# Perceiver block with a routed expert layer: six of eight inner slices of each looped expert's output as split products, and its copy out of PSUM moved to ScalarE

## The chip, the cores and the metric

The kernel runs on one core of a Trainium2 chip. The metric is the device time of one execution in microseconds (us); smaller is better. Of several runs the median counts.

## What is computed

The reference is one block of a perceiver on x of 8 x 64 x 512 with a context of 8 x 512 x 512, all in f32: a cross attention with its own output projection, a causal self attention (16 heads of 32) with a convolution over its output, and an expert layer. The expert layer is the part that matters here:

```
logits = x @ gate_w.T ; probs = softmax(logits) ; top2_p, top2_i = top_k(probs, 2)
w = top2_p / max(sum(top2_p), 1e-10)
hh = gelu(einsum('nd,edf->nef', x, w1) + b1)        # E = 14 experts, F = 1024
all_out = einsum('nef,efd->ned', hh, w2) + b2       # D = 512
moe = w[:, 0:1] * out0 + w[:, 1:2] * out1           # of the two chosen experts
x = x + clip(layernorm(x) + moe, -100, 100)
```

There are 512 tokens, so 1024 pairs of token and expert.

## The kernel before

Tokens are sorted by expert through a table in DRAM, `rows_dram`, in blocks of 128 rows. Each expert has at least one block; here there are 14 blocks, numbered b = 0 to 13, worked in pairs, u = b % 2 naming the buffer. For a block, TensorE turns the gathered rows (`turn_x`, L1901, with the transposes of L1522), multiplies them by w1 (`hidden`, L1906), turns the result so that the inner dimension of 1024 lies on partitions (`turn_hidden`, L1928, matmuls of L1933), and multiplies by w2 (`output`, L1936). The inner dimension comes in FT = 8 slices of 128.

An f32 product can be made in two ways. Unsplit it is one f32 matmul, which the profile counts as two instructions. Split it is three matmuls of the rounded type fp32r: high x high, high x low and low x high, where the high part is a copy of the tile to fp32r (ScalarE) and the low part the tile minus its high part (VectorE). The hidden products (L1920 to L1922) are all split. For outputs, blocks 0, 1 and the last are unsplit (L1943, L2002), and the others, 2 to 12, go through `split_output` (L1949): slices G to 7 unsplit (L1953) and slices 0 to G-1 split (L1958 to L1960), with G = 4. All of it adds up in one PSUM bank, YP.

The steady state is a loop over pairs on each engine. Within one iteration, for block b of the pair, the order is written out by hand:

- TensorE (L1984): turn_x(b), output(b-2), turn_hidden(b-1), hidden(b).
- ScalarE (L772): split_hi (L644, four high parts of w1 of block b, L648), high_w2 (L741, two high parts of w2 of block b-1, L746; it waits until that w2 has landed), store_y (L752: waits for y_taken, issues the store of block b-2 at L755), gelu (L726: eight activations of block b-1, L732, then the high part of its split slices, L739).
- VectorE (L1461): take_xT (L1334, L1336: high and low part of the turned x), split_lo (L1314, four low parts of w1, L1319), take_y (L1435: waits for y_psum and for y_free, then copies YP to ysb, L1438), low_w2 (L1422, two low parts, L1427), low_h (L1430, waits for the high part of h, L1432), take_h (L1402, two copies of the hidden result out of PSUM, L1407; waits for the end of hidden(b)).
- SyncE (L449) issues the loads: x rows of block b (L453) after turn_x(b-2), w2 of block b-2 (L446) when output(b-4) has ended, w1 of block b (L459) when hidden(b-2) has ended. A load of w1 or w2 is 2 MB.
- GpSimd issues the load of b1 (L881).

The semaphores that matter: y_psum counts ended outputs, y_taken the copies out of YP, y_free the stores of ysb that have landed, w2_high and w2_low the parts of w2, h_high and h_low those of h, hi_ready and lo_ready those of w1. TensorE waits in split_output for both w2_low of the block and for h_low behind the unsplit slices.

After the loop come output(12), with turn_hidden(13) placed inside it, the output of block 13 in two halves, and the gathers of all rows (L889) by GpSimd, which wait for the stores of the blocks. Block 13 is added from SBUF by a matmul with a matrix `last_w` that is made by VectorE during output(12).

Buffers are cut out of larger ones: w2_hi lies in wqkv_lo and c_hi, h_hi in A2r, last_w in wqkv, att and attT are tiles of their own from the cross attention.

Of the kernel before, what the change touches and what calls it, by code (L numbers as in the profile page):

```python
# [14 lines left out]
F32 = mybir.dt.float32  # L15
# [4 lines left out]
ALU = mybir.AluOpType  # L20
ACT = mybir.ActivationFunctionType
AX = mybir.AxisListType

P = 128
B, S = 8, 64
D = 512
Q = 512
KT = D // P
N = B * S
NT = N // P  # L30
# [3 lines left out]
FT = F // P  # L34
# [14 lines left out]
def perceiver_kernel(nc, t, out):  # L49

    ctx = ExitStack()
    with ctx:
        def sb(name, shape, dt=F32):
            return ctx.enter_context(nc.sbuf_tensor(name, shape, dt))

        def overlaid(name, rounded_name, shape):

            with nc.sbuf_tensor(name, shape, F32) as plain:
                pass
            return plain, sb(rounded_name, shape, F32R)  # L60

        def sem(name):
            return ctx.enter_context(nc.semaphore(name))
# [36 lines left out]
        w2, w2_lo = overlaid("w2", "w2_lo", [P, 2, FT * D])  # L100
# [11 lines left out]
        c_raw, c_hi = overlaid("c_raw", "c_hi", [P, KT, N])  # L112
# [10 lines left out]
        wqkv_flat = wqkv[:, :, :].rearrange("p k n -> p (k n)")  # L123
        wqkv_lo_flat = wqkv_lo[:, :, :].rearrange("p k n -> p (k n)")
        got = wqkv_flat[:, 0:2 * NT * D].rearrange("p (t c d) -> p t c d", t=NT, c=2)

        last_w = wqkv_flat[:, 4096:4608].rearrange("p (t s) -> p t s", t=NT)
        last_wT = wqkv_flat[:, 5120:5632].rearrange("p (t n) -> p t n", t=NT)
        A2, A2r = overlaid("A2", "A2r", [P, 3 * KT * N + KT * B * (S + 2)])
        zero_rows = A2[:, 7680:8192]  # L130
        cwT = A2[:, 0:2048].rearrange("p (k n) -> p k n", k=KT)
# [25 lines left out]
        hpre = A2[:, 2048:3072]  # L157
        hT = A2[:, 3072:5120].rearrange("p (u f n) -> p u f n", u=2, f=FT)
        ysb = A2[:, 5120:6144].rearrange("p (u d) -> p u d", u=2)
        att = sb("att", [P, Q])  # L160

        attT = sb("attT", [P, KT, P]); c2q = sb("c2q", [P, D])
        slot_row_i = c2q[:, 0:P].bitcast(I32); last_w2 = c2q[:, P:2 * P]
        over_e, over_r = (c2q[:, at:at + E * MORE] for at in (2 * P, 2 * P + P // 2))
        over_e_i, over_r_i = over_e.bitcast(I32), over_r.bitcast(I32)
# [21 lines left out]
        slot_c = sb("slot_c", [P, 2, E]); key = sb("key", [P, E, MORE]); base_slot = sb("base_slot", [P, 1])  # L187
        slot_k = sb("slot_k", [P, 2, NT]); slot_i = sb("slot_i", [P, 2, NT], I32)
        rank = sb("rank", [P, 2]); rel = sb("rel", [P, 2, NT]); early = sb("early", [P, 2, NT]); wgot = sb("wgot", [P, 2, NT])
        G = FT // 2  # L190
        w2_hi = [wqkv_lo_flat[:, 0:G * D], c_hi[:, :, :].rearrange("p k n -> p (k n)")[:, 0:G * D]]
        h_hi = A2r[:, 1024:2048].rearrange("p (u f n) -> p u f n", u=2, f=G)
        h_lo = A2r[:, 3072:5120].rearrange("p (u f n) -> p u f n", u=2, f=FT)[:, :, 0:G, :]
        c_hi_flat = c_hi[:, :, :].rearrange("p k n -> p (k n)")
        c_raw_flat = c_raw[:, :, :].rearrange("p k n -> p (k n)")
# [27 lines left out]
        HP, HT, XT, YP = (pb[0:2], pb[2:4]), pb[4:6], pb[6], pb[7]  # L223
# [58 lines left out]
        hT_psum, gelu_done, y_psum = map(sem, ("hT_psum", "gelu_done", "y_psum"))  # L282

        y_taken = sem("y_taken")
        gelu_half, h_high, h_low = sem("gelu_half"), sem("h_high"), sem("h_low")
        w2_high, w2_low = sem("w2_high"), sem("w2_low")

        y_free = [sem(f"y_free{u}") for u in range(2)]
# [68 lines left out]
        def rows_of(eng, b):  # L357

            return eng.value_load(blk_i[0:1, 1, bass.ds(b, 1)], min_val=0, max_val=ROW_BLOCKS - 1)
# [116 lines left out]
        def _(act):  # L476
# [249 lines left out]
            def gelu(b, u, loaded, first=False):  # L726

                act.wait_ge(hT_psum, b + 1)
                for f in range(FT):
                    if f == 0:  # L730
                        act.wait_ge(b1_in[u], loaded)
                    ins = nc.scalar.activation(hT[:, u, f, :], HT[f // 4][:, tile(f % 4)], ACT.Gelu,  # L732
                                               bias=b1_sb[:, u, f:f + 1])
                    if f == G - 1 and not first:
                        ins.then_inc(gelu_half, 1)
                ins.then_inc(gelu_done, 1)
                if not first:
                    act.wait_ge(gelu_half, b + 1)
                    nc.scalar.activation(h_hi[:, u], hT[:, u, 0:G, :], ACT.Copy).then_inc(h_high, 1)  # L739

            def high_w2(b, u, loaded):  # L741

                act.wait_ge(w2_in[u], loaded)
                for i in range(2):
                    at = slice(i * G * D // 2, (i + 1) * G * D // 2)
                    nc.scalar.activation(w2_hi[u][:, at], w2[:, u, at], ACT.Copy).then_inc(w2_high, 1)  # L746

            def store_first(b, u):
                act.wait_ge(y_taken, b + 2)
                act.dma_start(rows_dram[b * P:(b + 1) * P, :], ysb[:, u, :]).then_inc(y_free[u], 16)  # L750

            def store_y(b, u):  # L752
                row = rows_of(act, b)
                act.wait_ge(y_taken, b + 2)
                act.dma_start(rows_dram.rearrange("(b p) d -> b p d", p=P)[bass.ds(row, 1)]  # L755
                              .rearrange("o p d -> p (o d)"), ysb[:, u, :]).then_inc(y_free[u], 16)
# [5 lines left out]
            act.wait_ge(scattered, 16 * 2 * NT)  # L762
            store_first(0, 0)
            gelu(1, 1, 16, True)
            for count, n in ((gelu_half, 2), (h_high, 2), (w2_high, 4)):
                act.sem_inc(count, n)
            split_hi(1, w1_in[1], 16, range(2, KT))
            store_first(1, 1)
# [3 lines left out]
            with act.Fori(2, pairs) as i:  # L772
                for u in range(2):
                    split_hi(u, w1_in[u], 16 * i, range(KT))
                    if u == 0:
                        high_w2(2 * i - 1, 1, 16 * i)
                    else:
                        high_w2(2 * i, 0, 16 * i + 16)
                    store_y(2 * i - 2 + u, u)
                    if u == 0:  # L780
                        gelu(2 * i - 1, 1, 16 * i)
                    else:
                        gelu(2 * i, 0, 16 * i + 16)
# [115 lines left out]
        def _(dve):  # L899
# [521 lines left out]

            def low_w2(b, u):  # L1422

                for i in range(2):
                    dve.wait_ge(w2_high, 2 * b + i + 1)
                    at = slice(i * G * D // 2, (i + 1) * G * D // 2)
                    nc.vector.tensor_tensor(w2_lo[:, u, at], w2[:, u, at], w2_hi[u][:, at].bitcast(F32), ALU.subtract) \  # L1427
                        .then_inc(w2_low, 1)

            def low_h(b, u):  # L1430
                dve.wait_ge(h_high, b + 1)
                nc.vector.tensor_tensor(h_lo[:, u], hT[:, u, 0:G, :], h_hi[:, u].bitcast(F32), ALU.subtract) \  # L1432
                    .then_inc(h_low, 1)

            def take_y(b, u, turn):  # L1435
                dve.wait_ge(y_psum, b + 3)
                dve.wait_ge(y_free[u], 16 * turn)
                nc.vector.tensor_copy(ysb[:, u, :], YP[:, :]).then_inc(y_taken, 1)  # L1438
# [13 lines left out]
            split_lo(3, 1, range(KT))  # L1452
            take_xT(3, 1)
            take_y(1, 1, 1)
            for count, n in ((h_low, 2), (w2_low, 4)):
                dve.sem_inc(count, n)
            low_w2(2, 0)
            low_h(2, 0)
# [2 lines left out]
            with dve.Fori(2, pairs) as i:  # L1461
                for u in range(2):
                    take_xT(2 * i + u, u)
                    split_lo(2 * i + u, u, range(KT))
                    take_y(2 * i + u - 2, u, i)
                    low_w2(2 * i + u - 1, 1 - u)
                    low_h(2 * i + u - 1, 1 - u)
                    take_h(2 * i + u, u)
# [8 lines left out]
            for n in range(NT):  # L1477
# [4 lines left out]
                ins = nc.vector.tensor_tensor(last_w[:, n, :], last_w[:, n, :], last_w2[:, :], ALU.add)  # L1482
# [33 lines left out]
        def _(pe):  # L1516
            mm = nc.tensor.matmul
# [430 lines left out]

            def split_output(onto, b, u, at, width, between=None):  # L1949
                for f in range(G, FT):  # L1950
                    if between and f == G + 2:
                        between()
                    mm(onto, hT[:, u, f, :], w2[:, u, f * D + at:f * D + at + width], start=(f == G), stop=False)  # L1953
                pe.wait_ge(w2_low, 2 * b + 2)
                pe.wait_ge(h_low, b + 1)
                for f in range(G):
                    cols = slice(f * D + at, f * D + at + width)
                    mm(onto, h_hi[:, u, f, :], w2_hi[u][:, cols], start=False, stop=False)  # L1958
                    mm(onto, h_hi[:, u, f, :], w2_lo[:, u, cols], start=False, stop=False)
                    ins = mm(onto, h_lo[:, u, f, :], w2_hi[u][:, cols], start=False, stop=(f == G - 1))  # L1960
                return ins

            pe.sem_inc(y_psum, 2)
# [7 lines left out]
            for n in range(NT):  # L1971
                ins = nc.tensor.transpose(XT[0:E, tile(n)], wsel[:, n, :], ident[:, :])
# [21 lines left out]
            for n in range(NT):  # L1994
                ins = nc.tensor.transpose(XT[:, tile(n)], last_w[:, n, :], ident[:, :])
# [3 lines left out]
            for c in range(2):  # L1999
                for f in range(FT):  # L2000
                    at = f * D + c * D // 2
                    ins = mm(HALF[c], hT[:, 1, f, :], w2[:, 1, at:at + D // 2], start=(f == 0), stop=(f == FT - 1))  # L2002
                ins.then_inc(half_psum, 1)

            for n in range(NT):
# [3 lines left out]
                for c in range(2):  # L2009
                    if n == 0:  # L2010
# [3 lines left out]
                    ins = mm(pb[n][:, half], last_wT[:, n, :], ysb[:, 1, half], start=False, stop=True,  # L2014
                             skip_group_check=True)
# [43 lines left out]
```

## Time and profile before

| | us |
|---|---|
| median of 3 runs | 454.69 |
| lowest and highest of them | 451.72, 455.02 |
| the profiled execution, own time | 455.08 |
| its span, first to last instruction | 453.5 |
| busy in the span: TensorE, VectorE, ScalarE, GpSimd | 416.2, 320.4, 195.2, 66.4 |
| mean granted TensorE clock | 0.98 |

Busy times overlap; weight loads (PEld) run beside the matmuls (PE). The times of matmuls are modelled at their ends, so their issue distance is read from the chain of waits, where each piece lasts until the next one begins, and not from the mean of one. The chain is followed back from the last instruction to whatever released it.

### The profile page before, as it was taken

To read this page: it belongs to the slowest core of one execution; us is meant where nothing else is said; L and a number is where in the kernel's file an instruction comes from. 1 tells how busy PE (TensorE), PEld (TensorE's weight loads), DVE (VectorE), ACT (ScalarE), POOL (GpSimd) and SP (SyncE) were. 2 spreads that over 40 slices of the span, in tenths; PEclk is the share of its full clock that TensorE was granted. 3 is DMA by queue.
4 is the path that set the end of the run, shared out by engine and by line. 5 is a ranking of instruction groups with operands and counts; after the bars stand their busy time and mean duration, and the time that the engine had idled before them with its cause. 6 is when DMAs were issued, how large, how long until landed. Compare 5 with 4: busy or idle time off the path is not lost.

```text
span 453.5 us, 8173 instructions
## 1 busy us (share of the span) xinstructions
PE 416.2 (92%) x3051; PEld 311.3 (69%) x3060; DVE 320.4 (71%) x605; ACT 195.2 (43%) x347; POOL 66.4 (15%) x80
## 2 busy tenths in 40 slices
PE   1999999999999899997868999999999999999980
PEld 1666466689897798974547856777777777777740
DVE  5759787684189835428866986887888877778537
ACT  4236134123257143135226151957666667674200
POOL 2210000002216300211112500000000000000074
PEclk9999999999999899999889999999999999999996
DMA  7998798999902800047051559999999999994243
GB/s 257 401 375 330 243 417 332 408 408 407 399 17 49 300 4 3 1 159 309 1 185 73 204 176 397 343 353 353 354 356 367 390 365 354 359 339 152 96 142 136
DMA packets 50814, 116.95 MB, mean 258 GB/s; under 512 B 3266, under 2 KB 3282, under 8 KB 50784
## 3 DMA queue, kind: packets, MB, share of 16 engines
q1 hardware_dynamic: 38176, 92.28, 55.5%
q10 hardware_dynamic: 10592, 19.41, 11.2%
q0 software_dynamic: 2016, 4.84, 3.3%
q8 instruction: 21, 0.34, 0.3%
q14 instruction: 9, 0.07, 0.0%
HBM read 93.98 MB, written 21.50 MB: 255 GB/s over the span
## 4 chain that ended last, share of the span: by engine, by line
PE 80%; DVE 10%; issue 3%; POOL 2%; DMA 2%; ACT 2%; DVEq 0%; ACTq 0%; POOLq 0%
PE banks L1953 8%; PE banks L1920 5%; PE banks L1922 5%; PE banks L1921 5%; PE banks L1554 4%; PE banks L1556 3%; PE banks L1555 3%; PE banks L1541 3%; PE banks L1593 3%; PE banks L1522 3%; PE banks L1692 3%; PE banks L1770 3%; PE banks L1693 3%; PE banks L1694 3%; PE banks L1933 2%
## 5 line engine op out<-in xcount | busy, mean ns | idle before, releaser
L1319 DVE TENSOR_TENSOR w_lo<-w,w_hi 128x1024 fp32r<-128x1024 f32 x48 | 55.5, 1217 | 0.0
L648 ACT ACTIVATE w_hi<-w 128x1024 fp32r<-128x1024 f32 x48 | 47.4, 1096 | 2.3 <-DMA w<-in_w 2.3
L732 ACT ACTIVATE A<-banks,b_sb 128x128 f32<-128x128 f32 x112 | 30.4, 383 | 37.1 <-DVE A L1438 21.6
L1920 PE MATMUL banks<-w_hi,cT_r 128*128 128x512 f32 x100 | 40.1, 401 | 0.6 <-DVE cT_r L1336 0.6
L1953 PE MATMUL banks<-w,A 128*128 128x512 f32 x88 | 39.7, 592 | 0.0
L1922 PE MATMUL banks<-w_hi,cT_r 128*128 128x512 f32 x100 | 39.0, 390 | 0.0
L1921 PE MATMUL banks<-w_lo,cT_r 128*128 128x512 f32 x100 | 39.0, 390 | 0.0
L1407 DVE COPY A<-banks 128x512 f32<-128x512 f32 x28 | 18.0, 685 | 16.6 <-PE banks L1922 16.6
L1694 PE MATMUL banks<-A2r,w_lo 128*128 128x256 f32 x96 | 28.0, 292 | 0.0
L833 POOL TENSOR_TENSOR A<-A,hrec 128x1024 f32<-128x1024 f32 x8 | 17.0, 2128 | 70.1 <-DVE hrec L1159 70.1
L881 POOL DMA_DIRECT2D b_sb<-in_b1T x12 | 6.5, 542 | 140.8 <-ACT A L732 133.9
L1953 PEld LDWEIGHTS banks<-w,A 128*128 128x128 f32 x88 | 15.9, 190 | 15.4 <-issue 15.3
L1554 PE MATMUL banks<-w_lo,A2r 128*128 128x512 f32 x52 | 22.5, 433 | 2.1 <-DVE A2r L1017 2.1
L746 ACT ACTIVATE wqkv_lo<-w 128x1024 fp32r<-128x1024 f32 x12 | 12.1, 1053 | 23.7 <-DMA w<-in_w 14.5
L1920 PEld LDWEIGHTS banks<-w_hi,cT_r 128*128 128x128 f32 x100 | 18.8, 188 | 4.3 <-DVE cT_r L1336 0.9
L1922 PEld LDWEIGHTS banks<-w_hi,cT_r 128*128 128x128 f32 x100 | 18.8, 188 | 4.0
L1556 PE MATMUL banks<-w_lo,A2r 128*128 128x512 f32 x52 | 21.3, 409 | 0.0
L1555 PE MATMUL banks<-w_lo,A2r 128*128 128x512 f32 x52 | 21.3, 409 | 0.0
L1921 PEld LDWEIGHTS banks<-w_lo,cT_r 128*128 128x128 f32 x100 | 18.8, 188 | 3.5
L1150 DVE TENSOR_REDUCE hmax<-banks 128x16 f32<-128x1024 f32 x8 | 9.8, 1223 | 14.8 <-PE banks L1722 14.8
L1668 PE MATMUL banks<-c_hi,w_lo 128*128 128x256 f32 x64 | 18.6, 291 | 0.5 <-DVE A2r L1057 0.5
L1694 PEld LDWEIGHTS banks<-A2r,w_lo 128*128 128x128 f32 x96 | 18.9, 197 | 0.0
(332 smaller groups left out, 1027.8 us busy)
## 6 DMA issues: line engine op xcount, KB each, us to landing
w<-in_w SPq DMA_DIRECT2D x24, 2048.0 KB, 9.6
rows_dram<-A ACTq DMA_DIRECT2D x1, 14592.0 KB, 45.8
A<-in_ctxT SPq DMA_DIRECT2D x8, 1024.0 KB, 10.4
A<-in_ctx SPq DMA_DIRECT2D x8, 1024.0 KB, 9.5
w<-in_w SPq DMA_DIRECT2D x5, 1024.0 KB, 6.1
rows_dram<-A ACTq DMA_DIRECT2D x13, 256.0 KB, 6.8
w<-in_wlT SPq DMA_DIRECT2D x3, 1024.0 KB, 14.7
wqkv<-in_wqkvT SPq DMA_DIRECT2D x1, 3072.0 KB, 16.1
```

Of the source, the lines that this page charges most:

```text
L648: nc.scalar.activation(w1_hi[:, u, k * F:(k + 1) * F], w1[:, u, k * F:(k + 1) * F], ACT.Copy).then_inc(hi_ready, 1)
L732: ins = nc.scalar.activation(hT[:, u, f, :], HT[f // 4][:, tile(f % 4)], ACT.Gelu, bias=b1_sb[:, u, f:f + 1])
L1319: nc.vector.tensor_tensor(w1_lo[:, u, part], w1[:, u, part], w1_hi[:, u, part].bitcast(F32), ALU.subtract).then_inc(lo_ready, 1)
L1554: mm(Z[n][:, :], high[:, k, :], wl_hi[:, at, :], start=(part == 0 and k == 0), stop=False)
L1555: mm(Z[n][:, :], high[:, k, :], wl_lo[:, at, :], start=False, stop=False)
L1556: ins = mm(Z[n][:, :], low[:, k, :], wl_hi[:, at, :], start=False, stop=(part == 2 and k == KT - 1))
L1668: mm(onto, w_hi, c_hi[:, k, tokens], start=(k == 0), stop=False)
L1694: ins = mm(onto, conv_lo[:, KT * tap + k, tile(f)], high, start=False, stop=(tap == CONV_ORDER[-1] and k == KT - 1))
L1920: mm(HP[u][c][:, :], xr[:, 0, u, k, :], high[:, at], start=(i == 0), stop=False)
L1921: mm(HP[u][c][:, :], xr[:, 0, u, k, :], low[:, at], start=False, stop=False)
L1922: ins = mm(HP[u][c][:, :], xr[:, 1, u, k, :], high[:, at], start=False, stop=(i == KT - 1))
L1953: mm(onto, hT[:, u, f, :], w2[:, u, f * D + at:f * D + at + width], start=(f == G), stop=False)
```

## The change

For blocks 2 to 12, slices 0 to 5 are split (G = 6) and slices 6 and 7 stay unsplit. The high and low parts of w2 become three copies and three subtractions of 128x1024 per block (CH = 3) in place of two; the high and low part of h go from 128x512 to 128x768. TensorE waits for w2_low ahead of every second split slice, and not once for all. In the loop, the copy of YP to ysb goes from VectorE (take_y, between split_lo and low_w2) to ScalarE, in store_y, between high_w2 and gelu. The copies of blocks 0, 1 and 12 stay on VectorE. In the last split output, turn_hidden stands between the two unsplit slices and the split ones. The parts find room in other buffers: w2_hi in three pieces per u, h_hi of u = 1 over att, last_w in c_raw.

```diff
@@ buffers @@
-        last_w = wqkv_flat[:, 4096:4608].rearrange("p (t s) -> p t s", t=NT)
-        last_wT = wqkv_flat[:, 5120:5632].rearrange("p (t n) -> p t n", t=NT)
+        c_flat = c_raw[:, :, :].rearrange("p k n -> p (k n)")
+        last_w = c_flat[:, 0:512].rearrange("p (t s) -> p t s", t=NT)
+        last_wT = c_flat[:, 1024:1536].rearrange("p (t n) -> p t n", t=NT)
...
-        att = sb("att", [P, Q])
-
-        attT = sb("attT", [P, KT, P]); c2q = sb("c2q", [P, D])
+        att_f, att_r = overlaid("att_f", "att_r", [P, 2 * Q])
+        att = att_f[:, 0:Q]
+        attT = att_f[:, Q:2 * Q].rearrange("p (k n) -> p k n", k=KT); c2q = sb("c2q", [P, D])
...
-        G = FT // 2
-        w2_hi = [wqkv_lo_flat[:, 0:G * D], c_hi[:, :, :].rearrange("p k n -> p (k n)")[:, 0:G * D]]
-        h_hi = A2r[:, 1024:2048].rearrange("p (u f n) -> p u f n", u=2, f=G)
+        G = 3 * FT // 4
+        CH = G // 2
+        c_hi_all = c_hi[:, :, :].rearrange("p k n -> p (k n)")
+        w2_hi = [[A2r[:, 6144:7168], A2r[:, 7168:8192], wqkv_lo_flat[:, 4096:5120]],
+                 [c_hi_all[:, 0:1024], c_hi_all[:, 1024:2048], wqkv_lo_flat[:, 5120:6144]]]
+        h_hi = [v[:, 0:G * P].rearrange("p (f n) -> p f n", f=G) for v in (A2r[:, 1024:2048], att_r[:, :])]
@@ ScalarE @@
-                    nc.scalar.activation(h_hi[:, u], hT[:, u, 0:G, :], ACT.Copy).then_inc(h_high, 1)
+                    nc.scalar.activation(h_hi[u], hT[:, u, 0:G, :], ACT.Copy).then_inc(h_high, 1)
...
-                for i in range(2):
-                    at = slice(i * G * D // 2, (i + 1) * G * D // 2)
-                    nc.scalar.activation(w2_hi[u][:, at], w2[:, u, at], ACT.Copy).then_inc(w2_high, 1)
+                for i in range(CH):
+                    at = slice(2 * i * D, 2 * (i + 1) * D)
+                    nc.scalar.activation(w2_hi[u][i], w2[:, u, at], ACT.Copy).then_inc(w2_high, 1)
...
-            def store_y(b, u):
+            def store_y(b, u, turn=None):
                 row = rows_of(act, b)
+                if turn is not None:
+                    act.wait_ge(y_psum, b + 3)
+                    act.wait_ge(y_free[u], 16 * turn)
+                    nc.scalar.activation(ysb[:, u, :], YP[:, :], ACT.Copy).then_inc(y_taken, 1)
                 act.wait_ge(y_taken, b + 2)
...
-                    store_y(2 * i - 2 + u, u)
+                    store_y(2 * i - 2 + u, u, i)
@@ VectorE @@
-                for i in range(2):
-                    dve.wait_ge(w2_high, 2 * b + i + 1)
-                    at = slice(i * G * D // 2, (i + 1) * G * D // 2)
-                    nc.vector.tensor_tensor(w2_lo[:, u, at], w2[:, u, at], w2_hi[u][:, at].bitcast(F32), ALU.subtract) \
+                for i in range(CH):
+                    dve.wait_ge(w2_high, CH * b + i + 1)
+                    at = slice(2 * i * D, 2 * (i + 1) * D)
+                    nc.vector.tensor_tensor(w2_lo[:, u, at], w2[:, u, at], w2_hi[u][i].bitcast(F32), ALU.subtract) \
                         .then_inc(w2_low, 1)
...
-                    take_y(2 * i + u - 2, u, i)
@@ TensorE @@
                 for f in range(G, FT):
-                    if between and f == G + 2:
-                        between()
                     mm(onto, hT[:, u, f, :], w2[:, u, f * D + at:f * D + at + width], start=(f == G), stop=False)
-                pe.wait_ge(w2_low, 2 * b + 2)
+                if between:
+                    between()
                 pe.wait_ge(h_low, b + 1)
                 for f in range(G):
+                    if f % 2 == 0:
+                        pe.wait_ge(w2_low, CH * b + f // 2 + 1)
```

The counts that are set ahead of the loop (`sem_inc` of w2_high and w2_low) go from 4 to 2 * CH, and the three split matmuls read the pieces of w2_hi.

## Rows read from the trace of the kernel before

**Rows 1.** Busy time by stretch: the expert loop, then single blocks of it
```profile
core 0: us, PE busy (x) PEld busy (x) DVE busy (x) ACT busy (x) POOL busy (x), PEclk, DMA share, GB/s
288.50:425.50 137.00, 137.00 (x592) 99.74 (x591) 112.92 (x140) 86.49 (x158) 4.96 (x10) 1.00 0.91 333
314.46:327.44 12.98, 12.98 (x58) 9.50 (x57) 10.68 (x12) 8.48 (x17) 0.54 (x1) 1.00 1.01 362
353.40:366.38 12.98, 12.98 (x58) 9.50 (x57) 10.68 (x12) 8.49 (x17) 0.54 (x1) 1.00 0.94 356
```

**Rows 2.** The chain of waits through one block: start us, us, what
```profile
321.10 0.87 PE banks L1933 x8
...
327.44 0.44 PE banks L1522 x4
327.87 3.44 PE banks L1953 x8
331.31 0.23 PE banks L1958
...
331.77 0.24 PE banks L1960
...
334.08 0.87 PE banks L1933 x8
...
340.42 0.11 PE banks L1522
```

**Rows 3.** Costliest groups, all stretches: busy us, mean ns of one | idle before
```profile
L1953 PE MATMUL banks<-w,A 128*128 128x512 f32 x88 | 39.7, 592 | 0.0
L746 ACT ACTIVATE wqkv_lo<-w 128x1024 fp32r<-128x1024 f32 x12 | 12.1, 1053 | 23.7 <-DMA w<-in_w 14.5 <-DVE A L1438 9.1
L739 ACT ACTIVATE A2r<-A 128x512 fp32r<-128x512 f32 x11 | 7.5, 681 | 0.0
L487 ACT ACTIVATE cT<-banks 128x512 f32<-128x512 f32 x8 | 4.7, 594 | 26.7 <-PE banks L1522 26.7
L1427 DVE TENSOR_TENSOR w_lo<-w,wqkv_lo 128x1024 fp32r<-128x1024 f32 x10 | 11.8, 1216 | 0.0
```

**Rows 4.** ScalarE and VectorE in order of time, one block of the loop
```profile
332.09 2.01 ACT L746 ACTIVATE wqkv_lo<-w 128x1024 fp32r<-128x1024 f32 x2 [2.76 <-DMA w<-in_w]
335.83 2.17 ACT L732 ACTIVATE A<-banks,b_sb 128x128 f32<-128x128 f32 x8 [1.73 <-DVE A L1438]
337.84 0.68 ACT L739 ACTIVATE A2r<-A 128x512 fp32r<-128x512 f32 x1
334.54 0.69 DVE L1438 COPY A<-banks 128x512 f32<-128x512 f32 x1
335.14 2.35 DVE L1427 TENSOR_TENSOR w_lo<-w,wqkv_lo 128x1024 fp32r<-128x1024 f32 x2
338.56 0.69 DVE L1432 TENSOR_TENSOR A2r<-A,A2r 128x512 fp32r<-128x512 f32 x1 [1.06 <-ACT A2r L739]
340.45 0.69 DVE L1407 COPY A<-banks 128x512 f32<-128x512 f32 x1 [1.21 <-PE banks L1922]
```

**Rows 5.** Stretches of 0.65 us around the hole; landing of L446's loads
```profile
347.56:348.21 0.65, 0.65 (x6) 0.59 (x5) 0.65 (x3) 0.00 (x0) 0.00 (x0) 1.00 1.01 416
...
349.51:350.16 0.65, 0.65 (x5) 0.53 (x4) 0.65 (x1) 0.65 (x4) 0.00 (x0) 1.00 0.76 129
...
DMA to landing us min/median/max: 9.4/10.2/10.7
```

**Rows 6.** In order of time: entry of the loop, and its end
```profile
283.38 2.01 ACT L746 ACTIVATE wqkv_lo<-w 128x1024 fp32r<-128x1024 f32 x2 [9.14 <-DVE A L1438]
285.29 2.15 ACT L732 ACTIVATE A<-banks,b_sb 128x128 f32<-128x128 f32 x8
...
288.97 3.44 PE banks L1953 x8
...
425.51 0.69 DVE L1438 COPY A<-banks 128x512 f32<-128x512 f32 x1 [0.57 <-PE banks L1960]
```

More of the change, by code:

```diff
@@ L764, in _ @@
             gelu(1, 1, 16, True)
-            for count, n in ((gelu_half, 2), (h_high, 2), (w2_high, 4)):
+            for count, n in ((gelu_half, 2), (h_high, 2), (w2_high, 2 * CH)):
                 act.sem_inc(count, n)
@@ L1431, in low_h @@
                 dve.wait_ge(h_high, b + 1)
-                nc.vector.tensor_tensor(h_lo[:, u], hT[:, u, 0:G, :], h_hi[:, u].bitcast(F32), ALU.subtract) \
+                nc.vector.tensor_tensor(h_lo[:, u], hT[:, u, 0:G, :], h_hi[u].bitcast(F32), ALU.subtract) \
                     .then_inc(h_low, 1)
@@ L1454, in _ @@
             take_y(1, 1, 1)
-            for count, n in ((h_low, 2), (w2_low, 4)):
+            for count, n in ((h_low, 2), (w2_low, 2 * CH)):
                 dve.sem_inc(count, n)
@@ L1950, in split_output @@
                 for f in range(G, FT):
-                    if between and f == G + 2:
-                        between()
                     mm(onto, hT[:, u, f, :], w2[:, u, f * D + at:f * D + at + width], start=(f == G), stop=False)
-                pe.wait_ge(w2_low, 2 * b + 2)
+                if between:
+                    between()
                 pe.wait_ge(h_low, b + 1)
                 for f in range(G):
+                    if f % 2 == 0:
+                        pe.wait_ge(w2_low, CH * b + f // 2 + 1)
                     cols = slice(f * D + at, f * D + at + width)
-                    mm(onto, h_hi[:, u, f, :], w2_hi[u][:, cols], start=False, stop=False)
-                    mm(onto, h_hi[:, u, f, :], w2_lo[:, u, cols], start=False, stop=False)
-                    ins = mm(onto, h_lo[:, u, f, :], w2_hi[u][:, cols], start=False, stop=(f == G - 1))
+                    own = slice(f % 2 * D + at, f % 2 * D + at + width)
+                    mm(onto, h_hi[u][:, f, :], w2_hi[u][f // 2][:, own], start=False, stop=False)
+                    mm(onto, h_hi[u][:, f, :], w2_lo[:, u, cols], start=False, stop=False)
+                    ins = mm(onto, h_lo[:, u, f, :], w2_hi[u][f // 2][:, own], start=False, stop=(f == G - 1))
                 return ins
```

## The prediction

> **What bounds the kernel now.** Read the stretches first. In the expert loop, about 288.5 to 425.5 us, TensorE is busy for all 137.00 us at granted clock 1.00, and one block takes 12.98 us of which TensorE fills 12.98, VectorE 10.68 and ScalarE 8.48 [rows 1]. So one matmul less is time less, as long as nobody else becomes late. The DMA engines show shares of 0.94 and 1.01 in two such blocks, at 356 and 362 GB/s [rows 1], which is the second suspect. Then read the chain of waits: inside a block it never leaves TensorE. It runs through the turn of x (0.44), the unsplit slices of the output (3.44), twelve split products (331.31 to 334.08), the turn of the hidden tile (0.87) and the hidden products (334.95, which is 334.08 + 0.87, to 340.42) [rows 2]. Last come the groups, for the price of each copy [rows 3], and the order of one block on ScalarE and VectorE, for the room beside TensorE [rows 4].
>
> **The change part by part.** *TensorE.* An unsplit slice is one f32 matmul that the profile counts as two instructions: 88 for 11 blocks of 4 slices [rows 3], so the split path runs 11 times (blocks 2 to 12). Four such slices take 3.44, one 0.86 [rows 2]. Twelve split products take 334.08 - 331.31 = 2.77, one 0.231, the three of a slice 0.693 [rows 2]. Two slices of a block go over from 0.86 to 0.693: -0.334 per block, and 11 x 0.334 = 3.67 us. Bounds: if each product ran at the pace of the hidden products (5.47 us for 24, 0.228 [rows 2]), eighteen would take 4.10 in place of 4.16 and the gain would be 0.39 a block, 4.3 in all; if the six new products of a block took the 0.24 of the slowest one in the chain [rows 2], they would cost 1.44 against 1.72, 0.28 a block, 3.1 in all. I take 3.67, since the new products are the same line, shapes and buffers' kind as the twelve. The waits on w2_low, now three instead of one, cost nothing by the hidden products, which wait for lo_ready ahead of every six and still keep 0.228. The turn of the hidden tile in the last split output stays behind two unsplit slices (f = 6, 7 in place of 4, 5), as before.
>
> *ScalarE* gets per block a third copy of w2 (two take 2.01, one 1.05, so 0.96 more [rows 3, 4]), the copy out of PSUM and a longer high copy of h. A 128x512 copy out of PSUM takes 0.594 on ScalarE [rows 3] against 0.69 on VectorE [rows 4]. The high copy of h goes from 128x512 (0.681) to 128x768; between 0.681 and the 1.053 of 128x1024 I take 0.87 [rows 3]. Sum 8.48 + 0.96 + 0.60 + 0.19 = 10.23 of the new 12.65. *VectorE* loses the copy (0.69), gets a third subtraction (2.35 for two, 1.22 for one alone, so 1.13 more) and a low part of h of 128x768 (0.69 now, 1.22 for 1024 elements, 0.96 taken) [rows 3, 4]: 10.68 - 0.69 + 1.13 + 0.27 = 11.39 of 12.65. Both fit, with 2.4 and 1.25 us to spare; the order must fit too.
>
> *The added wait.* ScalarE now waits for y_psum ahead of gelu, but it waited already there for VectorE's copy through y_taken: L732's idle time ends with L1438 (1.73 us) [rows 4]. Behind it are queued the store, gelu, the high part of h and the next split of w1; VectorE waits for the high part of h, TensorE for both. The loop puts high_w2 ahead of the copy, and high_w2 waits for a transfer. That is where the move can cost. Take the block of [rows 4], with its output ending at 334.08 before, and at 333.75 counted from the previous block's output end (321.10) and the new period. w2 lands at 332.09; three copies end at 335.06; the PSUM copy ends at 335.66 (before: 335.23); gelu began 0.60 behind that copy's end, so 336.26, and takes 2.17 to 338.43; the high part begins 0.16 before that and ends 339.14; VectorE's low part begins 0.04 after that and ends at 340.14. The hidden products end at 333.75 + 6.34 = 340.09, and take_h, 0.03 behind them before, is then 0.05 behind. So VectorE's two idle gaps of 1.06 and 1.21 us shrink, the second to nothing, and TensorE needs the low part only after 340.09 + 0.44 + 1.72 = 342.25. That leaves 2.1 us. Before it was over 5, since four unsplit slices stood ahead. A take_h that is later by some tenths costs nothing: its reader comes a whole output later, and the first low part of w1 is made near 343.8, where the hidden products that read it begin at 347.3.
>
> *Queues.* SP's waits are unchanged, the SP loads are issued by TensorE's progress and so 0.33 closer together; the y store leaves ScalarE's queue some 0.8 us later against the output's end, and its buffer is needed two blocks on. *DMA.* A block moves 362 GB/s x 12.98 us = 4.70 MB. Ahead of the hole that each block has, the rate stands at 416 GB/s; then four pieces of 0.65 us are lower, down to 129, when w1 has nearly landed and the next w2 has only been issued [rows 5]. At 400 GB/s the 4.70 MB need 11.75 us, so 12.65 fits, and the hole gets shorter. From issue to landing w2 takes 9.4 to 10.7 us [rows 5].
>
> *Entry.* The first split block has less room. The copies of w2 begin at 283.38 and the chain of ScalarE follows them with no gap [rows 6]: gelu 0.96 later, ends 288.4, the high part 289.1, VectorE's low part 290.1. TensorE starts output 2 at 288.97 and wants the low part at 290.69. It holds by 0.6 us; if not, the loss is once, under 1 us. *End.* The store of block 12 and the gathers hang on the end of output 12 (y copy at 425.51, released by L1960 [rows 6]), so what the loop gains arrives at the end. Moving last_w to another buffer and the overlays of att cost no instruction.
>
> **Sum.** The profiled run took 455.08 (span 453.5 plus 1.58 around it) and stands 0.39 above the median of 454.69. 455.08 - 3.67 = 451.41; on the median's footing 451.0.
>
> **The rivals.** *DMA rate holds the period.* The shares near 1.00 [rows 1] say that the engines are never without a packet; if bytes and not requests set the pace, the period stays 12.98, TensorE gets waits of 0.33 a block at the split of w2 or w1, and the time stays at 454.7. Against it stands the hole in the rate and the 416 beside it [rows 5]. The Trainium skill (DMA: Bandwidth & Descriptors, Where 436 GB/s comes from) is this rival's best advocate: it says that between HBM and SBUF the HBM side binds at about 358 GB/s per core, below the fabric's 435. By that price a block could not go under 13.1 us and nothing would be gained; this trace disagrees wherever it shows 416.
>
> *Late gelu: slower.* Ring through ScalarE: output ends, w2 is issued and lands 10.99 later, copies 2.97, PSUM copy 0.60, gap 0.60, gelu 2.01 to the high part, 0.87, low part 1.0, then eighteen products 4.16: 23.2 us for two periods of 12.65 = 25.3. It binds when w2 lands 2.1 us later than now, and makes the kernel slower than before from 2.8 us later (26.0 for two of 12.98). Landings 3.7 later, near 13.9 from issue, give (23.2 + 3.7) / 2 = 13.45 a block and 454.7 + 10 x 0.47 = 459.4. For it: the loads come closer together on engines at share 1.00, and the copy out of PSUM, gelu and h all stand behind that landing now. Against: in ten blocks w2's landing never passed 10.7 [rows 5].
>
> *More than the sum.* The gain with the pace of the hidden products is 4.3, and the clock outside the loop could differ; 450.0 or less.
>
> **How the numbers follow.** Forecast 451.0 (-3.7, -0.8%): 0.65, its own range 449.8 to 452.6. DMA holds the period: 0.20 (454.7). Late gelu: 0.09. More than the sum: 0.06. A measurement here tells about 1% (4.5 us) from no change; the three runs of before lie 451.72 to 455.02 apart, so about a third of the forecast's chance falls past 1%: faster 0.21 + 0.06 = 0.27; same 0.44 + 0.19 = 0.63; slower 0.10 (late gelu and a little of the DMA case). The range takes the forecast with that scatter and the DMA case: 449.0 to 455.4.
>
> **What would show it.** Right: turns of x 12.65 us apart; the unsplit slices 1.72 in the chain, the eighteen products 4.16; TensorE without idle in the loop; ScalarE's L746 still waiting for DMA, then copying y at once, without a wait for y_psum; VectorE waiting about 1 us for the high part of h and hardly for the hidden products. Wrong: an idle time of L1958 or of the first hidden product with ScalarE or VectorE behind it (late gelu), landings past 12 us; or shorter holes in the DMA rate with periods still 12.98 (DMA rate).

## The result, and the profile after

| | before | after |
|---|---|---|
| median of 20 runs each, us | 453.08 | 448.20 |
| lowest, highest | 451.47, 455.44 | 446.73, 451.63 |
| profiled span | 453.5 | 448.7 |

The ratio is 0.9895 with a 95% interval of 0.9878 to 0.9911. That is 4.9 us faster, where 3.7 was forecast, and 448.2 lies 0.8 us under the low end of the range. The three runs that the forecast stood on had a median of 454.69; with twenty it is 453.08. All these executions ran in the same, faster state.

The stretches of the kernel after answer to [rows 1]: the loop from the unsplit slices of output 2 on, and three blocks of it.

```profile
core 0: us, PE busy (x) PEld busy (x) DVE busy (x) ACT busy (x) POOL busy (x), PEclk, DMA share, GB/s
289.50:414.96 125.46, 125.46 (x578) 98.25 (x577) 114.86 (x121) 101.41 (x171) 5.36 (x10) 1.00 0.96 353
302.12:314.71 12.59, 12.59 (x60) 9.87 (x59) 11.48 (x13) 9.53 (x18) 0.54 (x1) 1.00 1.00 364
314.71:327.30 12.59, 12.59 (x59) 9.87 (x59) 10.58 (x12) 9.33 (x17) 0.49 (x1) 1.00 1.02 388
327.30:339.88 12.58, 12.58 (x59) 9.86 (x59) 12.03 (x14) 10.77 (x19) 0.58 (x2) 1.00 0.99 364
```

TensorE is still busy all the time, and a block takes 12.59 us in place of 12.98. The rate of the DMA engines has gone up with it, from 356 and 362 GB/s in the two blocks of before to 364 to 388: it was not what held the period. The chain of one block, against [rows 2]:

```profile
327.30 1.72 PE banks L1958 x4
329.01 0.23 PE banks L1967
...
333.11 0.87 PE banks L1940 x8
333.98 0.23 PE banks L1927
...
339.44 0.44 PE banks L1529 x4
```

Two unsplit slices take 1.72 and the eighteen products 333.11 - 329.01 = 4.10 us, 0.228 each, in place of 0.231. ScalarE and VectorE in order of time, around the output that ends at 320.52 on TensorE, against [rows 4]:

```profile
319.93 2.01 ACT L750 ACTIVATE c_hi<-w 128x1024 fp32r<-128x1024 f32 x2 [2.65 <-DMA w<-in_w]
321.84 1.04 ACT L750 ACTIVATE wqkv_lo<-w 128x1024 fp32r<-128x1024 f32 x1
322.79 0.58 ACT L761 ACTIVATE A<-banks 128x512 f32<-128x512 f32 x1
323.97 2.18 ACT L736 ACTIVATE A<-banks,b_sb 128x128 f32<-128x128 f32 x8 [0.61 <-ACT A L761]
325.99 0.90 ACT L743 ACTIVATE att_r<-A 128x768 fp32r<-128x768 f32 x1
326.92 0.96 DVE L1440 TENSOR_TENSOR A2r<-A,att_r 128x768 fp32r<-128x768 f32 x1 [1.97 <-ACT att_r L743]
```

The copy (L761) begins at once behind the third high part: in this profile ScalarE never waits for y_psum, it waits for w2 to land. Gelu begins 3.45 us behind the output's end (2.81 a block later, at 335.92 against 333.11), where I had 2.51.

### The profile page after: what moved, and what is told of

It reads as the page before. It is cut to its first block, busy times and chain, and to the rows that moved or that the text cites. A ratio compares the mean times of both kernels' runs of the same rounds, so it can differ in the third digit from the quotient of the medians.

```text
span 448.7 us, 8270 instructions
## 1 busy us (share of the span) xinstructions
PE 412.6 (92%) x3073; PEld 315.4 (70%) x3082; DVE 328.9 (73%) x606; ACT 212.9 (47%) x368; POOL 66.7 (15%) x80
## 4 chain that ended last, share of the span: by engine, by line
PE 76%; DVE 11%; DMA 5%; issue 3%; POOL 2%; ACT 2%; SPq 0%; DVEq 0%; ACTq 0%; POOLq 0%
PE banks L1927 5%; PE banks L1929 5%; PE banks L1928 5%; PE banks L1958 4%; PE banks L1969 3%; PE banks L1968 3%; PE banks L1967 3%; DMA w<-in_wlT 3%; PE banks L1561 3%; PE banks L1699 3%; PE banks L1777 3%; PE banks L1700 3%; PE banks L1701 3%; PE banks L1563 3%; PE banks L1529 3%
## 5 line engine op out<-in xcount | busy, mean ns | idle before, releaser
L736 ACT ACTIVATE A<-banks,b_sb 128x128 f32<-128x128 f32 x112 | 30.5, 384 | 26.1 <-PE banks L1940 14.7
L1701 PE MATMUL banks<-A2r,w_lo 128*128 128x256 f32 x96 | 28.0, 291 | 0.0
L1958 PE MATMUL banks<-w,A 128*128 128x512 f32 x44 | 20.7, 593 | 0.0
L750 ACT ACTIVATE A2r<-w 128x1024 fp32r<-128x1024 f32 x12 | 12.1, 1052 | 16.5 <-DVE A L1446 9.1
L1699 PE MATMUL banks<-A2r,w_lo 128*128 128x256 f32 x64 | 18.6, 291 | 0.0
```

The costliest lines, as they stand in the source:

```text
L1699: mm(onto, w_hi, high, start=(tap == CONV_ORDER[0] and k == 0), stop=False)
L1701: ins = mm(onto, conv_lo[:, KT * tap + k, tile(f)], high, start=False, stop=(tap == CONV_ORDER[-1] and k == KT - 1))
```

## The end of the kernel

The two chains behind the last product of output 12. Before, in order of time:

```profile
425.14 0.25 PE banks L1960
425.39 0.03 issue
425.42 0.05 DVEq L1437
425.46 0.05 issue
425.51 0.70 DVE A L1438
...
426.36 4.60 DMA rows_dram<-A
```

After:

```profile
421.44 0.24 PE banks L1969
421.68 0.03 issue
421.71 0.05 DVEq L1445
421.75 0.45 issue
422.20 0.70 DVE A L1446
...
423.02 0.33 issue
423.34 2.61 DMA rows_dram<-A
```

The copy starts 0.52 us behind the product instead of 0.12, and the store is issued 1.14 us behind that instead of 0.85: 0.69 us lost in "issue", time in which the profile shows nothing waited for. But the store lands after 2.61 us in place of 4.60. With that the two spans add up. The first unsplit slice begins 0.54 later (289.51 against 288.97), from there to the last product's end it is 132.17 against 136.42 (-4.25), from there to the store's landing 4.27 against 5.57 (-1.30), and the rest is 0.20 longer: -4.81 for spans of 448.7 and 453.5. That is one execution against one. The first unsplit slice began at 286.45 and 288.03 in two more profiles of the changed kernel (e1, e13) and at 288.01 in one of the kernel before (e0), so what lies ahead of the loop varies by more than the terms at the end.

What ran while the store was landing stands in the DMA view of those stretches. First the kernel before, 426.4 to 428.5, when the store's packets run on q10; then 428.5 to 431.1:

```profile
q10 hardware_dynamic: 135, 0.25, 30.3%
q8 instruction: 1, 0.02, 6.0%
q14 instruction: 1, 0.01, 1.2%
```

```profile
DMA packets 9, 0.02 MB, mean 6 GB/s; under 512 B 1, under 2 KB 1, under 8 KB 9
```

135 of 144 packets run within 0.7 us; the nine that are left, one sixteenth of the store, come up to 2.6 us later. In the middle of the 135 lies one packet of 16 KB on q8, a fetch of instructions. After the change a fetch on either queue starts ahead of the store's packets (422.8 to 423.4, while no packet of the store runs):

```profile
q8 instruction: 1, 0.02, 14.3%
q14 instruction: 1, 0.01, 4.5%
```

## The experiments

**The loop's two parts, each alone.**

```diff
 # e2: the changed kernel, copy of YP back on VectorE
                     split_lo(2 * i + u, u, range(KT))
+                    take_y(2 * i + u - 2, u, i)
...
-                    store_y(2 * i - 2 + u, u, i)
+                    store_y(2 * i - 2 + u, u)
```

> G = 6, but the copy of YP stays on VectorE. Theory (TensorE's products make the time): the period is 12.59 as with both parts and the ratio to the kernel before is 0.989 to 0.992, as long as VectorE holds: its busy time goes to 10.68 + 1.13 + 0.27 = 12.1 of 12.59, with the wait for the high part of h 1 us behind, which is 13.1 and does not fit. So I expect VectorE to become the bound: TensorE shows idle time released by VectorE, period 12.7 to 13.1, ratio 0.993 to 1.003. Rival (the move to ScalarE was not needed): 0.989 to 0.991.

The ratio is 0.9880 (0.9843 to 0.9916), the median 448.66. A stretch of 100 us in its loop:

```profile
302.00:402.00 100.00, 100.00 (x463) 78.53 (x462) 96.67 (x105) 77.54 (x130) 4.28 (x8) 1.00 1.01 372
```

The period is 12.59, and my expectation was wrong: VectorE, at 96.67 of 100, keeps up. ScalarE without the copy makes the high part of h earlier, so that VectorE hardly waits for it (1.7 us in seven waits over this stretch). The wait of 1 us that I added to VectorE's busy time was no fixed cost. Once more:

> G = 6 with the copy of YP on VectorE once more, in five more rounds. Theory (the move to ScalarE is worth nothing, and the 0.7 us that ScalarE's and VectorE's late starts cost at the last copy and store in the changed kernel are missing here): ratio 0.987 to 0.989, at or below the changed kernel's 0.9895. Rival (the move brings a part of the gain): ratio 0.991 or more.

The ratio is 0.9879 (0.9844 to 0.9914), the median 448.56, as the theory said. So the split alone brings all of the gain that is measured. In both profiles the last copy starts 0.12 us behind the product and the store 0.85 behind that.

```diff
 # e3: the kernel before, the copy of YP in the loop by ScalarE in store_y, take_y taken out of VectorE's loop
-                    take_y(2 * i + u - 2, u, i)
...
-                    store_y(2 * i - 2 + u, u)
+                    store_y(2 * i - 2 + u, u, i)
...
```

> G stays 4, only the copy of YP in the loop goes to ScalarE. Theory (TensorE bound): period 12.98, ratio 0.999 to 1.001. Rival (a part of the gain comes from the move, for example by less work of VectorE beside TensorE's reads): the split products run at 0.228 in place of 0.231 us, period 12.94, ratio 0.998 or lower.

The period is 12.98 and the products stay at 0.231, as the theory said. Yet the ratio is 0.9947 (0.9923 to 0.9972): below the theory's, and no case for the rival, whose pace and period did not come. The gain is not in the loop: from the first unsplit slice of output 2 to the last product it takes 136.41 us, against 136.42. What differs in its profile is the last store, which landed 2.10 us after the issue.

**How large the step per slice is.**

```diff
 # e9: the changed kernel
-        G = 3 * FT // 4
+        G = FT // 4
```

> The changed kernel with G = 2: two slices split and six not. Theory (TensorE's products make the time): 6 x 0.86 + 6 x 0.231 = 6.55 us for an output in place of 6.21 with G = 4 and 5.82 with G = 6, period 13.31 to 13.33, ratio to the kernel before 1.006 to 1.010. Rival (the gain of G = 6 is not the slices'): ratio under 1.003.

```profile
302.35:315.65 13.30, 13.30 (x56) 9.13 (x55) 8.67 (x10) 7.92 (x16) 0.54 (x1) 1.00 0.98 341
```

The block takes 13.30, beside 13.31 to 13.33 worked out: +0.32 on 12.98. The ratio is 1.0027 (1.0004 to 1.0051), less than the 1.006 at least that I expected; up to the issue of the last store it is 3.6 us longer than the kernel before, and that store landed after 1.99 in place of 4.60 us, which takes 2.6 back if the first profile of before is the one to compare with.

**Why the products are faster.** Two kernels move the wait for w2_low:

```diff
 # e4, in the kernel before; e5 is the reverse in the changed kernel, one wait for all three parts
-                pe.wait_ge(w2_low, 2 * b + 2)
...
+                    if f % 2 == 0:
+                        pe.wait_ge(w2_low, 2 * b + f // 2 + 1)
```

> The kernel before with the wait for w2_low ahead of each second split slice, as the change has it. In the profiles the twelve split products of an output keep 0.231 us before and the eighteen keep 0.228 after. Theory A (the wait inside the stream makes the pace): twelve products in 2.73 to 2.74 us, period 12.94, ratio 0.999. Theory B (the share of unsplit slices ahead makes it): 2.77, period 12.98.

> The changed kernel with one wait for all three parts of w2 ahead of the split slices. Theory A (the waits make the pace): eighteen products take 4.16 us and the period is 12.64. Theory B: 4.10 and 12.59. The wait for all parts itself can cost nothing: the third low part of w2 is there a whole block ahead.

In e4 the products take 0.231 us and the period is 12.98; in e5 they take 0.228, the period is 12.59 and the ratio 0.9900 (0.9855 to 0.9945). The waits don't make the pace. e4's ratio is 0.9969 (0.9942 to 0.9997) with an unchanged loop (136.41 us), and its store landed after 2.13 us.

```diff
 # e11: the changed kernel with as many split slices as before
-        G = 3 * FT // 4
+        G = FT // 2
```

> The changed kernel with G = 4: as many slices split as before, but the high parts of w2 and h lie where the change put them, and the copy of YP is ScalarE's. Twelve products of an output take 0.232 us each before, eighteen take 0.228 after, six with G = 2 take 0.228 to 0.230. Theory C (the places of the operands in SBUF make the pace): 0.228 here, period 12.93 to 12.94, ratio 0.993 to 0.997. Theory B (four unsplit slices ahead make it): 0.232 and 12.98.

Twelve products take 2.77 us again in ten of eleven outputs, which is 0.231 each (the 0.232 in the expectations is this pace), the period is 12.98 and the ratio 0.9980 (0.9955 to 1.0004). So it isn't the places of the operands either. But theory B is not shown by that: with G = 2, six unsplit slices ahead, six products took 1.37 us, 0.228 each, and with G = 4 the first split output, block 2, takes 2.73, 0.228 a product, in each profile while the next nine take 2.77. What makes the pace stays open.

This run is also the plainest measure of the split, since it differs from the changed kernel by G alone. From the first unsplit slice of output 2 to the last product it takes 136.39 us, the changed kernel 132.17; timed side by side (e13, below) the medians are 452.90 and 449.19. With G = 2, 4 and 6 a block takes 13.30, 12.98 and 12.59.

**How near ScalarE is to its edge.**

```diff
 # e7_2 (e7_1 and e12: range(1)); writes to a buffer that is free in the loop
                 act.wait_ge(w2_in[u], loaded)
+                for i in range(2):
+                    nc.scalar.activation(wqkv_flat[:, 2 * i * D:2 * (i + 1) * D], w2[:, u, 0:2 * D], ACT.Copy)
```

> The changed kernel with two more copies of 128x1024 ahead of the high parts of w2 on ScalarE in every block, whose result nobody reads. They stand for a w2 that lands 1.9 to 2.0 us later and for a ScalarE that is busier by as much. ScalarE's block is 10.2 busy and 0.6 gap in the changed kernel, so 12.8 with them, above 12.59. Theory (my ring of the forecast, with 2.1 us to spare for TensorE and ScalarE just past full): period 12.7 to 12.8, ratio to the kernel before 0.990 to 0.993. Rival (there was less room than I worked out, since VectorE waits for the high part of h and has almost none of its own): period 13.0 or more, ratio 0.998 or more.

```profile
DVE A2r L1442 <- ACT A2r L743: 7.9, 4, 2.2
...
PEld banks L1960 <- ACT A L736: 2.4, 4, 0.9
PE banks L1960 <- ACT A L736: 1.5, 3, 0.6
```

These are its waits from 300 to 400 us (total, times, longest). The period goes up to 12.96 in the mean of ten blocks (12.67 to 13.38), just short of the rival's 13.0, and the ratio is 0.9998 (0.9970 to 1.0026), as the rival had it. TensorE waits at L1960, the first unsplit slice, for gelu, and its chain runs back through a load of w2 of 10.73 us: the ring of the forecast, closed at gelu and not at the low part of h.

> The changed kernel with one more copy of 128x1024 per block ahead of the high parts of w2 on ScalarE, nobody reads it. Two of them cost 0.39 us a block: TensorE then waited for gelu ahead of the unsplit slices. In the changed kernel gelu ends 5.0 us behind an output's end and TensorE asks for it at 6.8. Theory (1.8 us of room): one copy, 0.96 to 1.0 us, costs nothing, period 12.59, ratio 0.989 to 0.990. Rival (the ring is already closed): period 12.75 or more, ratio 0.994 or more.

The ratio is 0.9932 (0.9906 to 0.9959), above what the theory allowed, and its interval reaches the rival's 0.994, but all but the first of the blocks of its profile take 12.59. It was timed again beside the changed kernel:

> One more copy per block on ScalarE, again: its profile had the period 12.59, its median 450.6 and its ratio 0.9932 against 0.9895 of the changed kernel. Theory (one copy leaves the loop alone but uses up the room that other executions need, so that some of them are late): times spread further up than the changed kernel's, 448 to 453, median 1 to 2 us above it in this call. Rival (the difference was chance): the same median within 0.5 us.

> The changed kernel, timed beside the two others of this call. Theory: ratio 0.988 to 0.991, period 12.59, its last store whole 2.1 to 2.6 us after its issue, since the 16 KB fetch starts ahead of the store's packets, and the copy ahead of it 0.5 us behind the last product.

The ratio is 0.9912 (0.9883 to 0.9941) and the median 449.63, against 0.9893 (0.9864 to 0.9922) and 449.19 for the changed kernel. The medians are 0.44 apart, which is what the rival gave, and the intervals overlap: by the times a loss from one copy is not shown. The profiles show one. In e12 TensorE waits for the copies of block 13's hidden result (take_h, L1417), and at the entry of the loop, ahead of the first unsplit slice, for gelu (L736):

```profile
PE banks L1942 <- DVE A L1417: 0.8, 1, 0.8
PE banks L1960 <- ACT A L736: 0.4, 1, 0.4
```

In e7_1 these are 0.4 and 0.4 us, and the changed kernel's first profile has neither. From the first unsplit slice of output 2 to the last product it takes 133.73 us in e12 and 133.11 in e7_1, against 132.17 to 132.55 in the five profiles with G = 6, the copy on ScalarE and no extra copy (after, e1, e13, e5, e6).

Even without an extra copy TensorE waits in one place. Part of the changed kernel's chain in e1, in order of time:

```profile
410.69 0.79 ACT A2r L743
...
412.44 0.23 DVE A L1415
...
412.98 0.69 DVE A L1415
...
413.72 1.09 PE banks L1940 x8
```

The turn of the hidden tile of block 13 (L1940) waits for take_h, which is queued behind low_h, which waits for the high part of h. The same stretch is on the chain in e5, e6 and e13, and not in the first profile. It is worth 0.3 us: 132.52 in e1 and 132.46 in e13, against 132.17.

**The end.**

> The changed kernel once more, unaltered, for a second profile. Open from the first pair of profiles: the last y store landed 4.6 us after its issue before the change and 2.6 us after it, which is 2.0 of the 4.8 us between the two spans. Theory A (the landing is chance, the gain is the loop's alone): the period is 12.59 again, and the landing may be anything from 2.5 to 5 us. Rival B (the change makes the last store land sooner): 2.6 us again.

The span is 445.6, the period 12.59, the landing 2.56, and the 0.45 and 0.33 us of "issue" are there again, at the same places. One repeated landing does not tell theory A from rival B; e0 below bears on it.

```diff
 # e6: the changed kernel, also block 12's copy by ScalarE
-            store_y(2 * last, 0)
+            store_y(2 * last, 0, last + 1)
...
-            take_y(2 * last, 0, last + 1)
```

> The changed kernel, with the copy of block 12's output also on ScalarE. In the changed kernel's profile that copy begins 0.52 us behind the last product of output 12, against 0.12 before the change, and the store is issued 1.14 us behind it, against 0.85. Theory (VectorE is at the end of its making of last_w, and the late copy gives back the 0.33 us that output 12 gained): with the idle ScalarE the copy begins within 0.15 us, and the ratio to the kernel before is 0.001 below the change's, near 0.988 to 0.9885. Rival (both delays are chance, such as fetching of instructions): 0.989 to 0.990.

The ratio is 0.9882 (0.9848 to 0.9917): inside the first theory's figures, but the interval holds the rival's too. Its copy starts 0.39 us behind the last product, with an "issue" of 0.34 ahead of it, and not within 0.15. My reason was wrong: VectorE had ended last_w 0.6 us before its copy in the changed kernel, and ScalarE, idle, is late as well. What holds the engines back there is not shown: an 8 KB fetch of instructions (422.88 to 423.32) runs beside ScalarE's 0.33 us, but none beside VectorE's 0.45 us (from 421.75) or ScalarE's 0.34 us in e6.

> The kernel before once more, unaltered, for a second profile. The first profile's last y store landed 4.60 us after its issue; in five profiles of other versions, one of them with the loop of before, it landed after 2.1 to 3.0. Theory (4.6 was chance, and the distance of 4.8 us between the two first spans holds 2 us of it): 2 to 3 us here, period 12.98. Rival (it belongs to the kernel before): 4.6 again.

The period is 12.98 and the landing 3.51 us, so neither 2 to 3 nor 4.6. Two executions of one kernel landed 1.1 us apart.

```diff
 # e8: the kernel before, with four more waits that hold already
             pe.wait_ge(last_ready, 1)
+            pe.wait_ge(last_ready, 1)
...
```

> The kernel before with four repeated waits on TensorE behind output 12, which hold already: no work changes, only where TensorE's code lies. In the two profiles of the kernel before, a fetch of 16 KB of instructions on DMA queue 8 began 1.1 us behind the issue of the last y store, among its packets, and the last nine packets of the store came up to 1.5 and 2.6 us late; in two profiles with the same loop where it began at 1.8 the store was whole after 1.8. Theory (chance of code placement is worth 1 to 2 us at the end): if the fetch moves off the packets, the store lands after 1.8 to 2.2 us plus its receipt and the ratio is 0.995 to 0.998; if it stays, 0.999 to 1.001. Rival (the landing has nothing to do with the fetch): landing and fetch don't go together.

The fetch stayed, 0.9 us behind the issue of the store, the landing was 4.08, and the ratio 0.9994 (0.9966 to 1.0021), as foretold for that case. Put together:

| profile | start of the 16 KB fetch, from the store's issue | its own time | landing of the store |
|---|---|---|---|
| before | +1.12 | 2.03 | 4.60 |
| e8 | +0.93 | 1.71 | 4.08 |
| e0 (before) | +1.10 | 1.35 | 3.51 |
| e3, G = 4 | +1.77 | 1.09 | 2.10 |
| e4, G = 4 | +1.81 | 1.06 | 2.13 |
| after | -0.41 | 1.37 | 2.61 |
| e1 (after) | -0.19 | 0.96 | 2.56 |
| e2 | +0.28 | 1.21 | 2.95 |

Where nothing makes them late, the store's packets begin between +0.85 and +1.6. Where the fetch begins among them, nine packets are late and the landing is 3.5 to 4.6, longer the longer the fetch takes. Where it begins behind them it is 2.1, ahead of them 2.6 to 3.0. The nine further profiles fit: e9 and e11, with the fetch behind the packets, 1.99 and 2.10; the others, with it between -0.33 and +0.41, 2.5 to 3.0. No run moved the fetch alone (in e8 it stayed), so the cause is inferred from unlike builds and not shown by one edit. Nor do single landings give the medians: e3, e4 and e11 have the loop of before and landings of 2.10 to 2.13, and their ratios are 0.9947, 0.9969 and 0.9980.

## Why the prediction was wrong in size

The forecast was 451.0 and the measured median is 448.2. Of the 2.8 us between them 1.6 are the median of before, which three runs put too high, and 1.2 are the gain, 4.9 in place of 3.7.

**Right.** TensorE bounds the loop, and the steps from G = 2 to 4 to 6 show it. 11 outputs, two slices each, go over. TensorE has no idle time in the loop, and the DMA rate does not hold the period. ScalarE is released by the landing of w2 and not by y_psum, and VectorE's wait for the end of the hidden products goes to almost nothing (0.2 us in the loop). The 128x768 pieces took 0.89 and 0.96 (0.87 and 0.96 taken), the copy out of PSUM 0.58 (0.594), the sum for TensorE's unsplit slices 1.72 (1.72).

**The mis-sized term.** The products: 0.231 each, taken from the twelve of before "since the new products are the same line, shapes and buffers' kind". Eighteen took 4.10 and not 4.16. The gain of a block is 12.98 - 12.59 = 0.39 and not 0.334. Up to the last product it is 4.25 in the first profile and 3.9 and 4.0 by e1 and e13, and not 3.67. The bound that I gave from the hidden products, 0.39 a block, was the value. The trace of before already had the second pace for the same lines: in block 2 twelve products took 2.73 us and not 2.77.

**Two terms at the end that the forecast had at nothing.** "What the loop gains arrives at the end" was true, but the end itself changed: 0.69 us more from the last product to the issue of the store, in each of the three profiles of the changed kernel, and less from there to the landing, 2.56 to 2.75 us against 3.51 and 4.60. With the first profile's loop and e1's landing the sum is -4.25 + 0.69 - 2.0 = -5.6 by the first landing of before, -4.5 by that of e0, against a measured -4.8 (0.9895 of 453.08). For e2, without the 0.69 and with 2.95, it is -5.9 to -4.8, and the measured ratio of 0.988 is -5.4. The loop is the larger part by far; how the end shares in the medians is not shown by any one edit.

**The range.** It was counted from the median of three runs, 1.6 above that of twenty. From 453.08 the forecast would have been 449.4 and its low end 447.4.

**What the rivals got.** "More than the sum", given 0.06, is the case that came: its condition, the pace of the hidden products, held, and its 450.0 or less was met with the help of the lower median of before. The rival that the DMA rate holds the period did not come: the engines moved 388 GB/s in one block, and 372 over 100 us in e2. The Trainium skill's bound of about 358 GB/s per core for transfers between HBM and SBUF (DMA: Bandwidth & Descriptors, Where 436 GB/s comes from) does not hold in these traces. Late gelu did not come in the loop, but its room was smaller than the 2.1 us worked out: two copies, 1.9 us, closed it. The 2.1 us were counted from one block, to the moment when TensorE needs the low part of h; by the same figures gelu, which TensorE asks for ahead of the unsplit slices at 6.34 + 0.44 = 6.8 us behind the output's end, had 2.1 as well (338.43 against 340.53). What one block did not show is the scatter: gelu ended 4.2 to 5.6 us behind the output's end in the first profile and once 6.2 in e1, where a w2 took 11.7 us to land, past the 10.7 of before. That leaves 0.6 to 2.6 us. And at block 13, where only two unsplit slices and no output stand ahead of the turn of the hidden tile, take_h had no room: "End" had left that out.

**The move to ScalarE** was not weighed alone in the forecast. It was not needed: e2 and e10 without it are at 0.988.

## What to carry to other kernels

In a stretch where one engine is busy throughout, the gain is the change of that engine's own issue distance times the count; take the distance as a range if the trace shows two paces for the same instruction, because 0.003 us per product is 0.6 us over the 198 products of the eleven outputs. Compare the tails of two builds separately before crediting an edit: here the landing of the last store differed by up to 2 us between builds where the loop gained 3.9 to 4.3. Read the room of a chain from all blocks and not from one. Before moving work between engines, run the half without the move.

## What the runs showed that I had not expected

In three profiles a 16 KB fetch of instructions began among the packets of a 256 KB store, and one sixteenth of that store came 1.5 to 2.6 us late. VectorE was busy for 96.67 of 100 us in e2, in strict order beside a full TensorE, and cost it nothing. And a split product of unchanged form has two paces, 0.228 and 0.231 us, that changed with the number of split slices but neither with its waits nor with the place of its operands.
